# The middle attention of a two-layer graph network: a second buffer for transposed probabilities, and another order of the attention's units

## The chip, the cores and the metric

The program runs on one core of one Trainium2 chip. The metric is the device time of one execution in microseconds; several executions are timed, and their median is given. TensorE is called PE, VectorE DVE, ScalarE ACT, GpSimd POOL and SyncE SP, as in the profile.

## What is computed

The reference is a network of two layers over 625 nodes with 512 features and 20,625 edges. Each layer adds to x a graph convolution and a linear attention of its normalised input, and then a third block. The first layer's third block is the middle attention, an ordinary softmax attention over all nodes:

```python
q = (x @ wq).reshape(B, S, N_HEADS, D_K).transpose(0, 2, 1, 3)
scores = jnp.einsum('bhqd,bhkd->bhqk', q, k) / jnp.sqrt(jnp.float32(D_K))
attn = jax.nn.softmax(scores, axis=-1)
out = jnp.einsum('bhqk,bhkd->bhqd', attn, v)
return out.transpose(0, 2, 1, 3).reshape(B, S, D_MODEL) @ wo
```

It has 8 heads of 64 columns (a router picks one of three sets of weights, with 8, 4 or 1 heads of keys and values; the host repeats the columns, so that the device always computes 8). The second layer's third block multiplies the nodes by 128 matrices of 512 x 512, weighted by a softmax of distances; it takes the greater part of the time and isn't touched.

## The kernel before

All nodes stand as T = 5 tiles of P = 125 rows. Products are made in halves: an operand is split into an upper part (rounded to fp32r by ACT, names ending in h) and the rest (the difference, taken by DVE, names ending in l), and a product is three matmuls, upper by upper, upper by rest and rest by upper (L1698 to L1700).

Engines follow fixed lists written out by hand. A list of units (UNITS) sets the order in which PE fills PSUM. PSUM has four slots of two banks; unit n takes slot n % 4 (L125), and PE begins a unit when the unit that had the slot before it, four units earlier, is drained (L128 and `begin`). A unit is drained by ACT if it is a score (semaphore drained_s), and by DVE otherwise (drained_v). The semaphores count, so each engine has to keep to the order of the list.

In the middle attention there are 40 items, a tile of queries for a head each (item i is tile i % 5 of head i // 5), and three kinds of units:

- score i: six matmuls (64 rows, 314 columns) into a slot. DVE takes the negative maximum of each row (negmax, L1388), ACT the exponential into prob, which has four buffers (L967, with the sum of each row beside it), and this drains the slot. DVE corrects the sum for three padded columns (rowsum, L1393) and inverts it (rinv, L1396). POOL multiplies prob by rinv (L732).
- probT i: five transposes of prob, 125 x 125 each (L1920). ACT copies them to PTh (L978 for tiles 0 to 3, L807 for tile 4), DVE takes PTl (L1405 and, through the helper `rest`, L1124), and this drains the slot. ACT may write prob's buffer again for item i + 4 when probT i is in PSUM.
- attn h: for a head, 30 matmuls (125 rows, 314 columns) of PTh and PTl with VFh and VFl, when all five probT of the head are drained. ACT writes the result to XTh (L807), DVE to XTl (L1124), and this drains the slot.

PTh and PTl hold one head. `attention_steps(i)` gives the item whose score, the head whose product and the item whose transposes belong to step i. LAG = 2 puts the transposes two items behind the scores. The list is made from the steps, but where a step has an attention product, the scores of this and of the next step are put ahead of it, and their transposes behind it:

```python
        steps = (i, i + 1) if attention_steps(i)[1] is not None else (i,)
        for s, part in enumerate(("score", "attn", "probT")):
            ATTENTION += [(part, attention_steps(n)[s]) for n in steps if attention_steps(n)[s] is not None]
```

So PE's order around the first product is: score 6, probT 4, score 7, score 8, attn 0, probT 5, probT 6, score 9, probT 7. ACT goes through the same list, exponentials for the scores. DVE has a loop of its own (L1384): in pass i it does negmax of score i, rowsum and rinv of item i - 1, and then, for step i - 1, XTl of the head, if the step has one, and PTl of its item.

Ahead of the stage DVE pads PTh and PTl with zeros (L1382, L1383), and PE waits for it (pt_padded). Weights are loaded by SP into Wraw, one side of two (side 0 or 1), rounded by ACT into Wh (L817) and split by POOL into Wl (L687). The last weight split ahead of the stage is L1_q, on side 0. POOL does this before its first scaling. SP loads the next weights only behind the stage: the load of L1_k waits until the projection behind the attention is drained, and L1_v, the next for side 0, comes after it.

Behind the stage the projection proj1 multiplies XTh and XTl by the weight F_o, adds the result to X, and normalisation and the second layer follow.

Of the kernel before, what the change touches and what calls it, by code (L numbers as in the profile page):

```python
# [4 lines left out]
F32 = mybir.dt.float32  # L5
F32R = mybir.dt.float32r
# [3 lines left out]
ALU = mybir.AluOpType  # L10
ACT = mybir.ActivationFunctionType
# [63 lines left out]
    for i in range(n)]  # L75
UNITS += [(s + "0", i) for s, i in CONTEXT_AND_ROWS]

LAG = 2
UNITS += [("mean", 0), ("hidden", 0), ("logits", 0)] + [(s, i) for s, n in (("xt1", T), ("q1", K), ("k1", K), ("v1", 3)) for i in range(n)]
ITEMS = HEADS * T  # L80

# [1 line left out]
def attention_steps(i):  # L83


    done = i - LAG
    return (i if i < ITEMS else None, done // T - 1 if done > 0 and done % T == 0 else None,
            done if 0 <= done < ITEMS else None)

ATTENTION = []
for i in range(ITEMS + LAG + 1):
    if attention_steps(i - 1)[1] is None:
        steps = (i, i + 1) if attention_steps(i)[1] is not None else (i,)
        for s, part in enumerate(("score", "attn", "probT")):
            ATTENTION += [(part, attention_steps(n)[s]) for n in steps if attention_steps(n)[s] is not None]
UNITS += ATTENTION
UNITS += [("proj1", i) for i in range(3)]  # L100

# [79 lines left out]
def build(nc, A, out):  # L181
    with ExitStack() as ctx:
# [5 lines left out]


        X = sb("X", [P, T, D], F32)  # L190
        XN = sb("XN", [P, T, D], F32)
        XTh = sb("XTh", [128, K, NT], F32R)
        XTl = sb("XTl", [128, K, NT], F32R)
# [19 lines left out]
        with ExitStack() as s:  # L213
            sb("below_gat", [128, 3, K, D], F32, s)
            gatW = sb("gatW", [P, 3, CH, 128], F32, s)

        Wraw, Wh, Wl = ([None, None] for _ in range(3))
        for i in (1, 0):
# [1 line left out]
        rows = sb("rows", [P, 4, D], F32)  # L220
        ident = sb("ident", [128, 128], F32)
        ones = sb("ones", [128, 64], F32)
        onesr = sb("onesr", [128, 64], F32R)
        stats = sb("stats", [P, T, 6], F32)
        meanvar = sb("meanvar", [P, T, 2], F32)
        rstd = sb("rstd", [P, T], F32)
# [69 lines left out]
        with ExitStack() as s:  # L296
            QFh = sb("QFh", [128, K, NT], F32R, s)
            QFl = sb("QFl", [128, K, NT], F32R, s)
            KFh = sb("KFh", [128, K, NT], F32R, s)
            KFl = sb("KFl", [128, K, NT], F32R, s)  # L300
            VFh = sb("VFh", [P, T, D], F32R, s)
            VFl = sb("VFl", [P, T, D], F32R, s)
            PTh = sb("PTh", [P, T, NT], F32R, s)
            PTl = sb("PTl", [P, T, NT], F32R, s)
            prob = sb("prob", [P, 4, NT], F32, s)

        with ExitStack() as s:
            K2h = sb("K2h", [P, T, D], F32R, s)
# [165 lines left out]

        def slot(unit):
            return PS[:, 2 * SLOT[unit]:2 * SLOT[unit] + 2, :]

        def name_of(w):
            return WEIGHTS[w][0]
# [319 lines left out]
        def _(act):  # L799
# [155 lines left out]
            for m, tiles in enumerate(TILES):  # L955
                u = ("v1", m)
                wait_filled(u)
                upper(u, VFh[:, tiles[0]:tiles[-1] + 1], slot(u)[0:P, 0:len(tiles), :])
            weight_upper(WEIGHT["L1_q"])
            for part, n in ATTENTION:  # L960
                if part == "score":
                    item = n
                    u = ("score", item)
                    act.wait_ge(max_ready, item + 1)
                    if item >= 4:
                        act.wait_ge(filled, NUMBER[("probT", item - 4)] + 1)
                    a.activation(halves(prob[:, item % 4]), slot(u)[0:P, :, 0:HN], ACT.Exp, bias=negmax[:, item:item + 1],  # L967
                                 accum_out=rowsum[:, item:item + 1]).then_inc(drained_s, 1)
                if part == "attn":
                    head = n  # L970
                    u, o = ("attn", head), 64 * (head % 2)
                    wait_filled(u)
                    upper(u, halves(XTh[o:o + 64, head // 2]), slot(u)[o:o + 64, :, 0:HN])
                if part == "probT":
                    turned = n
                    u, c = ("probT", turned), tile_columns(turned % T)
                    wait_filled(u)
                    a.activation(PTh[:, 0:4, c], slot(u)[0:P, 0, 0:4 * P].rearrange("p (k n) -> p k n", k=4), ACT.Copy)  # L978
                    upper(u, PTh[:, 4, c], slot(u)[0:P, 1, 0:P])


            layer_std(2)
# [106 lines left out]
        def _(dve):  # L1089
# [289 lines left out]
            for m, tiles in enumerate(TILES):  # L1379
                u, j = ("v1", m), slice(tiles[0], tiles[-1] + 1)  # L1380
                rest(u, VFl[:, j], slot(u)[0:P, 0:len(tiles), :], VFh[:, j])
            v.memset(PTh[:, :, N:NT].bitcast(F32), 0.0)  # L1382
            v.memset(PTl[:, :, N:NT].bitcast(F32), 0.0).then_inc(pt_padded, 1)  # L1383
            for i in range(ITEMS + LAG + 2):  # L1384
                if i < ITEMS:
                    u = ("score", i)
                    wait_filled(u)
                    v.tensor_reduce(negmax[:, i:i + 1], slot(u)[0:P, :, 0:HN], AX.XY, ALU.max, negate=True).then_inc(max_ready, 1)  # L1388
                if 1 <= i <= ITEMS:

                    n = i - 1
                    wait_drained(dve, ("score", n))
                    v.scalar_tensor_tensor(out=rowsum[:, n:n + 1], in0=prob[:, n % 4, N - 1:N], scalar=float(N - NT),  # L1393
                                           in1=rowsum[:, n:n + 1], op0=ALU.mult, op1=ALU.add).then_inc(sum_ready, 1)
                    dve.wait_ge(sum_ready, n + 1)
                    v.reciprocal(rinv[:, n:n + 1], rowsum[:, n:n + 1]).then_inc(rinv_ready, 1)  # L1396

                _, head, turned = attention_steps(i - 1)
                if head is not None:
                    u, o = ("attn", head), 64 * (head % 2)  # L1400
                    rest(u, halves(XTl[o:o + 64, head // 2]), slot(u)[o:o + 64, :, 0:HN], halves(XTh[o:o + 64, head // 2]))
                if turned is not None:
                    u, c = ("probT", turned), tile_columns(turned % T)
                    dve.wait_ge(upper_ready, splits(u))
                    v.tensor_tensor(PTl[:, 0:4, c], slot(u)[0:P, 0, 0:4 * P].rearrange("p (k n) -> p k n", k=4),  # L1405
                                    PTh[:, 0:4, c].bitcast(F32), ALU.subtract)
                    rest(u, PTl[:, 4, c], slot(u)[0:P, 1, 0:P], PTh[:, 4, c])
            for m, tiles in enumerate(TILES):
                u, j = ("proj1", m), slice(tiles[0], tiles[-1] + 1)
                wait_filled(u)  # L1410
# [276 lines left out]
        def _(pe):  # L1687
# [201 lines left out]
            for part, n in ATTENTION:  # L1889
# [12 lines left out]
                if part == "attn":  # L1902
                    head = n
                    u, c = ("attn", head), slice(head // 2 * 128, head // 2 * 128 + 128)
                    begin(u)
                    wait_drained(pe, ("probT", T * head + T - 1))
                    for h in range(2):
                        queries = slice(h * HN, (h + 1) * HN)
                        for t in range(T):
                            ins = product(slot(u)[:, h, 0:HN], (VFh[:, t, c], VFl[:, t, c]), (PTh[:, t, queries], PTl[:, t, queries]),  # L1910
                                          t == 0, t == T - 1)
                    finish(ins)
                if part == "probT":
                    turned = n
# [216 lines left out]
```

## Time and profile before

| what | value |
|---|---|
| runs | 2633.29, 2635.6, 2635.8 us; median 2635.6 |
| profiled execution, its own time | 2621.18 us |
| its span, first to last instruction | 2619.2 us |
| middle attention, first score to first matmul of proj1 | 413.8 to 554.8 us |
| mean granted clock of TensorE over the span | 0.95 |

The profile is of one execution. Its page gives busy times by engine and the span in 40 equal slices of 65 us, with the granted clock in tenths; the trace behind it can be asked for the busy times of a stretch, for the waits of a stretch and for the instructions in order of time. Times of instructions are in us from the start of the span. TensorE's matmuls are pipelined: one starts before the one ahead of it has ended. A granted clock of 1.00 is 2.4 GHz, 0.50 is 1.2 GHz, and a value between is a mean of stretches at either.

### The profile page before, as it was taken

The numbers are of one execution on the slowest core, as the hardware profiler recorded it, in microseconds if no ns is written. First come the engines' busy times: TensorE is split into PE (matmuls) and PEld (weight loads), VectorE is DVE, ScalarE is ACT, GpSimd is POOL, SyncE is SP. The second block draws the span as 40 slices with busy tenths as digits, with TensorE's granted clock in tenths as the row PEclk, the third lists the DMA queues.
The fourth block names the chain that finished last, engine by engine and source line by source line (L and its number), as shares of the span: only waits on it lengthen the run. The fifth ranks groups of instructions, "written<-read, shape, count | busy, mean of one in ns | idle before, by whom it ended". The sixth has DMA issues, their size and how long they took to land.

```text
span 2619.2 us, 34595 instructions
## 1 busy us (share of the span) xinstructions
PE 2457.5 (94%) x11680; PEld 2056.2 (79%) x11680; DVE 1802.2 (69%) x2675; ACT 924.4 (35%) x1128; POOL 1649.6 (63%) x724
## 2 busy tenths in 40 slices
PE   6989978976899679999999999999999999999999
PEld 6878877865799667777777777777777777777777
DVE  8974324547588657777777777777777777777775
ACT  3732224522389552223223232223222322322231
POOL 0024322228888745777777777777777777777773
PEclk9989877988799779999999999999999999999999
DMA  3024010011433200221212212122122221221211
GB/s 77 16 68 162 17 65 17 1 49 47 110 87 92 79 38 33 97 84 76 96 64 96 95 65 96 69 91 96 64 96 80 80 96 64 96 91 69 96 64 36
DMA packets 49889, 190.90 MB, mean 73 GB/s; under 512 B 13300, under 2 KB 17911, under 8 KB 33444
## 3 DMA queue, kind: packets, MB, share of 16 engines
q1 hardware_dynamic: 35728, 177.90, 19.4%
q0 software_dynamic: 13200, 10.75, 1.9%
q10 hardware_dynamic: 900, 1.44, 0.2%
q8 instruction: 37, 0.61, 0.1%
q14 instruction: 24, 0.20, 0.0%
HBM read 177.54 MB, written 12.35 MB: 72 GB/s over the span
## 4 chain that ended last, share of the span: by engine, by line
PE 79%; DVE 10%; POOL 6%; issue 2%; ACT 2%; DMA 1%; SPq 0%; DVEq 0%; ACTq 0%; POOLq 0%
PE PS L1698 25%; PE PS L1700 25%; PE PS L1699 25%; POOL gatW L751 3%; POOL XN L751 2%; PE PS L1776 2%; DVE hotS L1151 1%; POOL gat L751 1%; DVE hotD L1152 1%; DVE negmax L1388 1%; DVE PTl L1405 1%; PE PS L1962 1%; PE PS L1920 0%; PE PS L1963 0%; DVE XN L1115 0%
## 5 line engine op out<-in xcount | busy, mean ns | idle before, releaser
L1648 DVE SCALAR_TENSOR_TENSOR XN<-PS,attn,XN 125x512 f32<-125x512 f32 x1083 | 805.4, 749 | 439.9 <-PE PS L1700 431.4
L789 POOL TENSOR_TENSOR OPl<-TS,OPh 128x1024 fp32r<-128x1024 f32 x256 | 677.5, 2647 | 116.7 <-ACT OPh L1061 116.7
L789 POOL TENSOR_TENSOR OPl<-RAW,OPh 128x1024 fp32r<-128x1024 f32 x192 | 555.2, 2892 | 273.4 <-ACT OPh L1061 273.4
L1698 PE MATMUL PS<-OPh,XTh 128*125 128x512 f32 x1280 | 507.6, 397 | 2.0 <-DVE attn L1602 2.0
L1700 PE MATMUL PS<-OPh,XTl 128*125 128x512 f32 x1280 | 506.1, 395 | 0.0
L1699 PE MATMUL PS<-OPl,XTh 128*125 128x512 f32 x1280 | 503.7, 394 | 0.0
L1061 ACT ACTIVATE OPh<-TS 128x1024 fp32r<-128x1024 f32 x256 | 271.8, 1062 | 530.0 <-PE PS L1700 517.3
L1061 ACT ACTIVATE OPh<-RAW 128x1024 fp32r<-128x1024 f32 x192 | 203.8, 1062 | 579.1 <-PE PS L1700 579.1
L1698 PE MATMUL PS<-OPh,Sh 128*125 128x512 f32 x1024 | 404.3, 395 | 3.1 <-DVE XN L1645 3.1
L1700 PE MATMUL PS<-OPh,Sl 128*125 128x512 f32 x1024 | 403.4, 394 | 0.0
L1699 PE MATMUL PS<-OPl,Sh 128*125 128x512 f32 x1024 | 402.1, 393 | 0.0
L1699 PEld LDWEIGHTS PS<-OPl,XTh 128*125 128x125 f32 x1280 | 238.7, 187 | 60.4
L1700 PEld LDWEIGHTS PS<-OPh,XTl 128*125 128x125 f32 x1280 | 238.0, 186 | 61.2
L1698 PEld LDWEIGHTS PS<-OPh,XTh 128*125 128x125 f32 x1280 | 237.5, 186 | 60.1 <-DVE attn L1602 2.2
L687 POOL TENSOR_TENSOR Wl<-Wraw,Wh 128x2048 fp32r<-128x2048 f32 x15 | 69.2, 4615 | 255.0 <-ACT Wh L817 254.9
L1698 PEld LDWEIGHTS PS<-OPh,Sh 128*125 128x125 f32 x1024 | 189.5, 185 | 50.6 <-issue 3.9
L1962 PE MATMUL PS<-hotE,msgh 125*128 125x314 f32 x660 | 201.5, 321 | 28.8 <-DVE msgl L1506 21.6
L1700 PEld LDWEIGHTS PS<-OPh,Sl 128*125 128x125 f32 x1024 | 190.0, 186 | 48.1
L1699 PEld LDWEIGHTS PS<-OPl,Sh 128*125 128x125 f32 x1024 | 190.1, 186 | 47.7
L1963 PE MATMUL PS<-hotE,msgl 125*128 125x314 f32 x660 | 198.9, 316 | 0.0
L1962 PEld LDWEIGHTS PS<-hotE,msgh 125*128 125x128 f32 x660 | 130.2, 197 | 32.5 <-issue 29.1
L751 POOL DMA_INDIRECT gatW<-nodes,dstI x90 | 134.8, 1497 | 29.0 <-issue 27.1
(345 smaller groups left out, 3587.6 us busy)
## 6 DMA issues: line engine op xcount, KB each, us to landing
RAW<-in_values SPq DMA_DIRECT2D x64, 2048.0 KB, 7.5
filters<-filt SPq DMA_DIRECT2D x14, 672.0 KB
fil<-filters SPq DMA_DIRECT2D x11, 840.0 KB
Wraw<-in_ffn SPq DMA_DIRECT2D x4, 1024.0 KB, 5.3
Wraw<-in_L_q SPq DMA_DIRECT2D x2, 1024.0 KB, 5.1
Wraw<-in_L_k SPq DMA_DIRECT2D x2, 1024.0 KB, 8.7
Wraw<-in_L_v SPq DMA_DIRECT2D x2, 1024.0 KB, 7.3
gatW<-nodes,dstI POOLq DMA_INDIRECT x90
```

The lines of the kernel that those rows point to most:

```text
L687: g.tensor_tensor(Wl[SIDE[w]][:], Wraw[SIDE[w]][:], Wh[SIDE[w]][:].bitcast(F32), ALU.subtract).then_inc(w_split, 1)
L751: g.indirect_dma_start(gats[c % RING][:, u, :], None, nodes, bass.IndirectOffsetOnAxis(ap=dstI[:, t:t + 1], axis=0)).then_inc(gathered[c % ...
L789: g.tensor_tensor(OPl[:, j], operand_source(j, parity), OPh[:, j].bitcast(F32), ALU.subtract).then_inc(op_lower, 1)
L1061: a.activation(OPh[:, j], operand_source(j, parity), ACT.Copy).then_inc(op_upper, 1)
L1151: v.tensor_scalar(hotS[:, parity, u, :], iota16[:, 0:N + 1], srcF[:, bass.ds(t, 1)], None, ALU.is_equal)
L1648: v.scalar_tensor_tensor(out=XN[:, t], in0=PS[0:P, bank, :], scalar=w, in1=XN[:, t], op0=ALU.mult, op1=ALU.add).then_inc(v_added, 1)
L1698: mm(dst, lh, rh, start=start, stop=False, skip_group_check=resumed)
L1699: mm(dst, lh, rl, start=False, stop=False, skip_group_check=resumed)
L1700: return mm(dst, ll, rh, start=False, stop=stop, skip_group_check=resumed)
L1776: ins = mm(PS[0:P, count_bank(n), 0:HALF], hotS[:, parity, u, s * P:(s + 1) * P], hotD[:, parity, u, 0:HALF], start=(c == m * COUNT_CHUNKS ...
L1962: mm(dst, msgh[:, q, u, c_], hot, start=(first and u == 0), stop=False)
L1963: ins = mm(dst, msgl[:, q, u, c_], hot, start=False, stop=(last and u == EB - 1))
```

## The change

1. LAG is 3, and the product of a head belongs to the step one later than before: its five probT come three items behind the scores, and the product one item behind the last of them.
2. The pairs of scores are gone: every step is score, attn, probT. The order around the first product is: score 7, probT 4, score 8, probT 5, score 9, attn 0, probT 6, score 10, probT 7, score 11.
3. PTh and PTl have two buffers. Even heads use PTh and PTl, odd heads PTh_odd and PTl_odd for tiles 0 to 3, and PTh_odd4 and PTl_odd4 for tile 4. PTh_odd lies over XN, which isn't in use in the stage. PTh_odd4 and PTl_odd4 lie over Wraw of side 0. So ACT (ahead of its first exponential) and DVE (ahead of the padding) wait until L1_q is split. To make room onesr has 2 columns instead of 64 (two are used).
4. DVE pads both buffers, with eight memsets instead of two. Its loop is one pass longer.

```diff
-LAG = 2
+LAG = 3
 def attention_steps(i):
-    done = i - LAG
-    return (i if i < ITEMS else None, done // T - 1 if done > 0 and done % T == 0 else None,
-            done if 0 <= done < ITEMS else None)
-ATTENTION = []
-for i in range(ITEMS + LAG + 1):
-    if attention_steps(i - 1)[1] is None:
-        steps = (i, i + 1) if attention_steps(i)[1] is not None else (i,)
-        for s, part in enumerate(("score", "attn", "probT")):
-            ATTENTION += [(part, attention_steps(n)[s]) for n in steps if attention_steps(n)[s] is not None]
+    turned = i - LAG
+    behind = turned - 1
+    return (i if i < ITEMS else None, behind // T - 1 if behind > 0 and behind % T == 0 else None,
+            turned if 0 <= turned < ITEMS else None)
+ATTENTION_STEPS = ITEMS + LAG + 2
+ATTENTION = [(part, n) for i in range(ATTENTION_STEPS)
+             for part, n in zip(("score", "attn", "probT"), attention_steps(i)) if n is not None]
...
         X = sb("X", [P, T, D], F32)
+        with ExitStack() as s:
+            PTh_odd = sb("PTh_odd", [P, T - 1, NT], F32R, s)
         XN = sb("XN", [P, T, D], F32)
...
+        with ExitStack() as s:
+            sb("below_PT", [128, 3, K, D], F32, s)
+            PTh_odd4 = sb("PTh_odd4", [P, NT], F32R, s)
+            PTl_odd4 = sb("PTl_odd4", [P, NT], F32R, s)
...
-        onesr = sb("onesr", [128, 64], F32R)
+        onesr = sb("onesr", [128, 2], F32R)
...
+        def prob_turned(head):
+            if head % 2:
+                return (PTh_odd[:], PTh_odd4[:]), (PTl_odd[:], PTl_odd4[:])
+            return (PTh[:, 0:T - 1], PTh[:, T - 1]), (PTl[:, 0:T - 1], PTl[:, T - 1])
...
             weight_upper(WEIGHT["L1_q"])
+            act.wait_ge(w_split, WEIGHT["L1_q"] + 1)
             for part, n in ATTENTION:
...
-            v.memset(PTh[:, :, N:NT].bitcast(F32), 0.0)
-            v.memset(PTl[:, :, N:NT].bitcast(F32), 0.0).then_inc(pt_padded, 1)
-            for i in range(ITEMS + LAG + 2):
+            dve.wait_ge(w_split, WEIGHT["L1_q"] + 1)
+            for head in range(2):
+                for first, last in prob_turned(head):
+                    v.memset(first[:, :, N:NT].bitcast(F32), 0.0)
+                    ins = v.memset(last[:, N:NT].bitcast(F32), 0.0)
+            ins.then_inc(pt_padded, 1)
+            for i in range(ATTENTION_STEPS + 1):
```

The copies on ACT, the subtractions on DVE and the matmuls of the product take their tiles from `prob_turned` instead of from PTh and PTl, in the same shapes.

## Rows read from the trace of the kernel before

**Rows 1.** The page: TensorE's busy time and granted clock in 40 slices

```profile
PE 2457.5 (94%) x11680; PEld 2056.2 (79%) x11680; DVE 1802.2 (69%) x2675; ACT 924.4 (35%) x1128; POOL 1649.6 (63%) x724
...
PEclk9989877988799779999999999999999999999999
```

**Rows 2.** Busy times by engine and granted clock (PEclk), by head

```profile
core 0: us, PE busy (x) PEld busy (x) DVE busy (x) ACT busy (x) POOL busy (x), PEclk, DMA share, GB/s
...
420.40:438.50 18.10, 17.62 (x61) 14.86 (x61) 9.25 (x28) 8.49 (x22) 4.66 (x7) 0.50 0.00 0
...
455.70:470.60 14.90, 13.29 (x85) 11.72 (x85) 9.79 (x28) 8.39 (x21) 4.12 (x6) 1.00 0.01 2
...
485.20:501.50 16.30, 14.85 (x85) 13.26 (x86) 9.67 (x27) 8.39 (x21) 3.98 (x6) 0.90 0.00 0
...
501.50:516.10 14.60, 13.33 (x85) 11.76 (x85) 9.51 (x27) 8.26 (x21) 3.93 (x5) 1.00 0.01 2
...
532.40:547.20 14.80, 11.27 (x61) 10.28 (x61) 7.06 (x19) 5.85 (x15) 2.40 (x4) 0.76 0.00 1
```

**Rows 3.** The waits of the stretch 413 to 556 us

```profile
PE PS L1698 <- DVE PTl L1124: 6.9, 8, 1.8
```

**Rows 4.** All engines in order of time, the start of the stage

```profile
413.65 0.07 DVE L1383 MEMSET PTl<- 125x15 f32 x1
...
413.77 0.40 PE L1698 MATMUL PS<-KFh,QFh 64*125 64x314 f32 x1 [1.46 <-DVE PTl L1383]
...
414.82 4.53 POOL L687 TENSOR_TENSOR Wl<-Wraw,Wh 128x2048 fp32r<-128x2048 f32 x1 [9.22 <-ACT Wh L817]
...
420.61 1.38 PE L1920 MATMUL PS<-ident,prob 125*125 125x125 f32 x5 [3.98 <-POOL prob L732]
```

**Rows 5.** PE in order of time at half clock, and the first attention product

```profile
431.53 0.62 PE L1698 MATMUL PS<-KFh,QFh 64*125 64x314 f32 x1
...
433.39 1.41 PE L1920 MATMUL PS<-ident,prob 125*125 125x125 f32 x5
...
434.73 0.62 PE L1698 MATMUL PS<-KFh,QFh 64*125 64x314 f32 x1
...
436.46 0.46 PE L1698 MATMUL PS<-KFh,QFh 64*125 64x314 f32 x1
...
438.69 0.60 PE L1698 MATMUL PS<-PTh,VFh 125*128 125x314 f32 x1 [0.46 <-DVE PTl L1124]
...
445.69 1.25 PE L1920 MATMUL PS<-ident,prob 125*125 125x125 f32 x10
```

**Rows 6.** PE in order of time at full clock, a product and what follows

```profile
470.64 0.38 PE L1698 MATMUL PS<-PTh,VFh 125*128 125x314 f32 x1 [0.76 <-DVE PTl L1124]
...
475.07 1.25 PE L1920 MATMUL PS<-ident,prob 125*125 125x125 f32 x10
...
476.26 0.40 PE L1698 MATMUL PS<-KFh,QFh 64*125 64x314 f32 x1
...
477.31 0.81 PE L1920 MATMUL PS<-ident,prob 125*125 125x125 f32 x5
...
478.05 0.41 PE L1698 MATMUL PS<-KFh,QFh 64*125 64x314 f32 x1
```

**Rows 7.** ACT and DVE in order of time behind the same product

```profile
475.27 0.69 ACT L807 ACTIVATE XTh<-PS 64x628 fp32r<-64x628 f32 x1 [3.16 <-PE PS L1700]
...
475.99 0.80 DVE L1124 TENSOR_TENSOR XTl<-PS,XTh 64x628 fp32r<-64x628 f32 x1 [4.52 <-ACT XTh L807]
...
477.50 0.79 DVE L1388 TENSOR_REDUCE negmax<-PS 125x1 f32<-125x628 f32 x1
...
478.48 0.66 DVE L1405 TENSOR_TENSOR PTl<-PS,PTh 125x500 fp32r<-125x500 f32 x1
...
479.25 0.80 DVE L1388 TENSOR_REDUCE negmax<-PS 125x1 f32<-125x628 f32 x1
```

**Rows 8.** PE in order of time, the last transposes

```profile
542.93 0.88 PE L1920 MATMUL PS<-ident,prob 125*125 125x125 f32 x5 [1.47 <-POOL prob L732]
```

More of the change, by code:

```diff
@@ L305, in build @@
             prob = sb("prob", [P, 4, NT], F32, s)
+            PTl_odd = sb("PTl_odd", [P, T - 1, NT], F32R, s)
         with ExitStack() as s:
@@ L977, in _ @@
                     wait_filled(u)
-                    a.activation(PTh[:, 0:4, c], slot(u)[0:P, 0, 0:4 * P].rearrange("p (k n) -> p k n", k=4), ACT.Copy)
-                    upper(u, PTh[:, 4, c], slot(u)[0:P, 1, 0:P])
+                    (first, last), _ = prob_turned(turned // T)
+                    a.activation(first[:, :, c], slot(u)[0:P, 0, 0:4 * P].rearrange("p (k n) -> p k n", k=4), ACT.Copy)
+                    upper(u, last[:, c], slot(u)[0:P, 1, 0:P])
             layer_std(2)
@@ L1404, in _ @@
                     dve.wait_ge(upper_ready, splits(u))
-                    v.tensor_tensor(PTl[:, 0:4, c], slot(u)[0:P, 0, 0:4 * P].rearrange("p (k n) -> p k n", k=4),
-                                    PTh[:, 0:4, c].bitcast(F32), ALU.subtract)
-                    rest(u, PTl[:, 4, c], slot(u)[0:P, 1, 0:P], PTh[:, 4, c])
+                    (first_h, last_h), (first_l, last_l) = prob_turned(turned // T)
+                    v.tensor_tensor(first_l[:, :, c], slot(u)[0:P, 0, 0:4 * P].rearrange("p (k n) -> p k n", k=4),
+                                    first_h[:, :, c].bitcast(F32), ALU.subtract)
+                    rest(u, last_l[:, c], slot(u)[0:P, 1, 0:P], last_h[:, c])
             for m, tiles in enumerate(TILES):
@@ L1906, in _ @@
                     wait_drained(pe, ("probT", T * head + T - 1))
+                    (first_h, last_h), (first_l, last_l) = prob_turned(head)
                     for h in range(2):
@@ L1909, in _ @@
                         for t in range(T):
-                            ins = product(slot(u)[:, h, 0:HN], (VFh[:, t, c], VFl[:, t, c]), (PTh[:, t, queries], PTl[:, t, queries]),
-                                          t == 0, t == T - 1)
+                            right = (last_h[:, queries], last_l[:, queries]) if t == T - 1 else (first_h[:, t, queries], first_l[:, t, queries])
+                            ins = product(slot(u)[:, h, 0:HN], (VFh[:, t, c], VFl[:, t, c]), right, t == 0, t == T - 1)
                     finish(ins)
```

## The prediction, made before the changed kernel ran

> **What bounds the kernel now.** I read the page first: TensorE is busy 94% of the span, and the granted clock falls below full in the first 15 of the 40 slices only [rows 1]. The change touches one stage there, the middle attention. The busy times cut at the beginnings of the attention products (438.5, 455.7, 470.6, 485.2, 501.5, 516.1, 532.4, 547.2 us) give one head per stretch [rows 2]. Three heads at full clock take 14.6 to 14.9 us, with PE 13.3 us busy (two of them are in the rows); two that hold a stretch of half clock (0.90 granted; one is in the rows) take 16.3. From 420.4 to 438.5 the clock is 0.50 throughout, though PE is busy for 17.6 of 18.1 us. So PE is nearly the bound, and what counts is its few gaps and the clock they leave behind. The list of waits names the largest regular one: eight attention products wait 6.9 us in all for the last PTl on VectorE [rows 3].
>
> **The change, part by part.**
>
> **1. The start.** The new buffers for the fifth tile lie over Wraw[0], so VectorE's padding now waits until POOL has split L1_q, and PE waits for the padding. POOL's split runs from 414.82 to 419.35; today the first score starts at 413.77, well before [rows 4]. After the change it starts at about 419.8: the end of the split, then eight small memsets (the one shown takes 0.07 us, and they overlap) and two semaphores. ScalarE waits for the same split; even if it loads its table of exponentials only then, that lies beside the first score and its maximum. Today PE has done three scores by 416.6 and waits until 420.61 for the first transposes [rows 4]. After, it has done none by 419.8, but has no gap from there on: with three scores ahead, the first transposes find their probabilities ready. It runs at half clock, as it does today from 420.4, because it stood idle for longer.
>
> At half clock a score takes 1.86 us ahead of transposes (431.53 to 433.39), some 1.70 ahead of another score (434.73 to 436.46), and five transposes take 1.34 [rows 5]. Ahead of the first attention product now stand ten scores and six transposes: 4 x 1.70 + 6 x 1.86 + 6 x 1.34 = 26.0 us, so it begins at 445.8, not 438.7: **7.1 us later**. One score and one set of transposes in that are work brought forward.
>
> **2. A head at full clock.** Call the end of an attention product 0, and let it be the one behind score 9. At full clock the product takes 4.43 us (470.64 to 475.07), five transposes behind it 0.60 (ten took 1.19), a score 1.05, transposes behind a score 0.74 [rows 6]. VectorE's item is 1.75 us (negmax to negmax; 0.98 of it for negmax, rowsum and rinv, 0.77 for PTl), XTl is 0.80 and ScalarE's XTh ahead of it 0.69 [rows 7]. Now the order. PE issues transposes 6, score 10, transposes 7, score 11. PSUM has four slots in turn, so score 11 takes the slot of the attention product, and that is free when VectorE has written XTl. VectorE's list for that step says negmax of score 10 first, then rowsum, rinv, and only then XTl. Before the change the extra score of the pair stood ahead of the product, so its maximum was taken while the product ran, and XTl came first. Without pairs: score 10 is complete at 0.60 + 1.05 + 0.10 = 1.75; negmax, rowsum and rinv 0.98, XTl 0.80 give 3.53 (XTh is done long before); with 0.15 of semaphore, as from VectorE's XTl at other places, score 11 starts at 3.7. PE was through with transposes 7 at 0.60 + 1.05 + 0.74 = 2.4. That is **a new PE gap of 1.3 us, once a head, right behind the product**. The double buffer does let VectorE do one more PTl during the product, but four items and XTl remain before the next one: 3.53 + 0.77, a wait for score 11 to 4.85, three items of 1.75 and one or two short waits of 0.2 to 0.3 for slots, so 10.3 to 10.7. With the product 14.7 to 15.2 a head, against 14.6 to 14.9. On the timetable alone the second buffer earns nothing, because the slot and the order of VectorE's list take back what it gives.
>
> **3. The clock.** What prices the gap is the clock. In the head from 420.4 to 438.5, PE issued scores and transposes without a break at half clock, and the clock did not come back; it came back during the attention product that followed [rows 2, 5]. At full clock PE waited 0.76 us ahead of six products, as in rows 6, and the clock fell at three of these, one of them in the head of 0.90 [rows 2]; it fell again in the last head, where the gap between transposes was 1.47 us and the granted clock of the head 0.76 [rows 2, 8]. The new gap is 1.3 us, close to the last, and lies among the same kind of work, scores and transposes. So I expect the clock to fall once behind each product, near the gap, and then to stay at half, since nothing but scores and transposes follows until the next product. Today the fall comes just before a product and is repaired by it within 3 to 4 us, for 1.4 to 1.7 us a time; after the change it comes at the other end of the head, and PE, not VectorE, sets the pace.
>
> The Trainium skill, TensorE: Matmul & The Clock Gate, "A second HAM failure mode: psum-queue depth-cycling", tells of a kernel that cycled through its PSUM banks and waited briefly between groups of matmuls, whose clock went back and forth; its rule gives the sum below, and its absence the first rival's. This trace agrees with it so far as one gap can show it.
>
> **The sum.** A head in that state: 3.7 us to score 11, which I leave at full clock (1.05), then three scores and three transposes at half clock, 3 x 1.86 + 3 x 1.34 = 9.6, less 0.16 since the last score has no transposes behind it: 14.2, and 14.1 for what still runs fast. The product, half of it slow, took 7.0 us in the first head (438.69 to 445.69) [rows 5]; where the fall came at its start a head was 1.6 us longer, so 6.0. I take 6.4. Head: **20.5 us**. Six of these from product 0 to product 6: 123.0, against 93.9 today (438.5 to 532.4). From product 6 to product 7 all probabilities are already scaled: product 6.4, XTh 0.7, XTl 0.8, four PTl 3.2, semaphores 0.2, so 11.3 against 14.8 [rows 2]. Behind product 7 nothing changes. Sum: 7.1 + (123.0 - 93.9) + (11.3 - 14.8) = **+32.7 us**.
>
> Costed at nothing: the shrunken onesr (two of its columns are all that is read); the other addresses of PTh and PTl (same shapes, same engines); SyncE, whose next load into Wraw[0] is L1_v, queued behind the wait for the last proj1, after the attention; POOL, which scales in the same order and is idle for most of the stage.
>
> The profiled execution took 2621.18 us (span 2619.2), the median of the runs is 2635.6, 14.4 us more. I carry the difference over to the median and take 32 of it for runs whose clock falls otherwise today: **2668 us**.
>
> **Rivals.**
>
> *The clock holds.* For: at full clock PE is still busy most of the time around the new gap, and three of six gaps of 0.76 us did nothing. Against: 1.47 us was enough once. Then only the timetable counts: product 0 at +7.1; the first interval 17.2 + 0.5, five of 15.2 (76.0), two falls as today 3.2, which brings product 6 to 542.7; then 4.4 + 5.0 to product 7 at 552.1, against 547.2. So +5, or +2 without any fall: 2637 to 2641. If it falls in some heads only, each that is spared gives back 20.5 - 15.2 = 5.3 us: two to four spared make 2647 to 2657.
>
> *Faster.* The place is score 11's slot. If it were free in time, VectorE (9.6 us a head) would no longer stand before PE, whose own work is 5 x 1.79 + 4.43, less 0.15, 13.2 us. Then product 1 comes 15.6 behind product 0, five more at 13.2, then 9.4: 445.8 + 15.6 + 66.0 + 9.4 = 536.8, against 547.2, or -10: 2625. It decides this way only if XTl is done by 2.4 us behind the product's end, and by rows 6 and 7 it is done at 3.53. The Trainium skill, Trainium Kernel Development and Optimization, "Best Practices", advises double buffers for performance; by it this rival would be the likely one, but in its sense PSUM's slots and VectorE's order would have to be widened too.
>
> *The start costs less.* If the split of L1_q ended earlier than in this trace, the first product would come up to 4 us sooner. That is a term of the forecast's own range and has no effect on the sign.
>
> **How the numbers follow.** Half clock behind nearly every product: 0.78, at +32 with its own range 2657 to 2674 (one or two heads spared below; every head 0.5 longer and the runs' own spread above). Some heads spared, 2647 to 2657: 0.07. The clock holds: 0.11. Faster: 0.04. The range from 2649 to 2674 leaves out the last two and a little of each end. A measurement of this kernel can tell about 0.2% (5.3 us) from no change: faster 0.04, the clock that holds gives 0.09 of no change and 0.02 of slower, so slower is 0.87.
>
> **What would show it.** Right: the first score near 419.8 and the first product near 446; a wait of PE for XTl of about 1.3 us some seven times, as scores (L1698) released by DVE XTl; granted clock about 0.65 over the stage; products some 20.5 us apart; the stage ending some 32 us later, nothing else moved. Wrong: products 15 us apart at a clock near 0.95 (the first rival), or no wait for XTl and PE without gaps (the second). An unexpected wait of an exponential for its prob buffer would mean that I misread the order of the lists.

## The result and the profile after

| | before | after |
|---|---|---|
| median of the runs, us | 2634.4 (4 runs) | 2664.9 (4 runs) |
| ratio of the times, 95% interval | | 1.0133 [1.0105, 1.0161] |
| profiled execution, its own time, us | 2621.2 | 2674.3 |
| mean granted clock over its span | 0.950 | 0.931 |
| last weight load of the stage ahead to first matmul of proj1, us | 411.7 to 554.8 (143.2) | 422.1 to 600.3 (178.1) |
| first attention product behind that weight load, us | 27.0 | 33.7 |
| product 0 to product 6, us | 93.8 | 124.4 |
| product 6 to product 7, us | 14.8 | 11.0 |

The changed kernel is 30.5 us slower by the medians. The forecast was 2668 with a range from 2649 to 2674. The weight load belongs to the last matmul of the stage ahead, which starts 0.2 us behind it; below, "the stage" is counted from this load to the first matmul of proj1. TensorE's busy time and its granted clock on the page, against [rows 1]:

```profile
PE 2506.8 (94%) x11680; PEld 2098.6 (79%) x11680; DVE 1800.7 (67%) x2681; ACT 924.2 (35%) x1128; POOL 1654.0 (62%) x724
...
PEclk9988777669699887999999999999999999999999
```

TensorE has as many instructions as before and is busy 49 us longer: the same work at a lower clock. The eighth and ninth slice (468 to 601 us) show a clock of 6 and 6, where those of before (458 to 589 us) show 9 and 8. The busy times by head (the columns are those of [rows 2]; the first stretch runs from the first score to product 0, the last from product 6 to product 7):

```profile
core 0: us, PE busy (x) PEld busy (x) DVE busy (x) ACT busy (x) POOL busy (x), PEclk, DMA share, GB/s
430.00:455.80 25.80, 25.75 (x90) 22.21 (x90) 13.11 (x35) 12.89 (x31) 6.32 (x8) 0.50 0.00 1
455.80:476.50 20.70, 19.57 (x87) 17.21 (x86) 9.77 (x26) 8.26 (x21) 3.95 (x5) 0.66 0.00 0
476.50:497.30 20.80, 19.52 (x86) 17.24 (x85) 9.98 (x26) 8.38 (x21) 3.95 (x5) 0.66 0.00 1
580.30:591.30 11.00, 8.60 (x52) 8.27 (x51) 6.01 (x16) 4.12 (x11) 1.58 (x2) 0.81 0.00 0
```

A head that took 14.6 to 17.2 us takes 20.6 to 20.9, with the same 85 or so matmul records. PE is idle for 1.1 to 1.3 us of it, no more than the 1.3 to 1.6 of before; but the clock is 0.66 where it was 0.83 to 1.00. PE's waits in the stage name the idle time (the engine and line that waits, what it waited for; total, times, longest):

```profile
PE PS L1716 <- DVE PTl_odd L1399: 7.3, 1, 7.3
PE PS L1716 <- DVE XTl L1137: 7.2, 6, 1.3
PE PS L1716 <- DVE PTl_odd L1137: 2.4, 1, 2.4
```

The eight waits for the last PTl ahead of a product [rows 3] are gone but for one of 2.4 us ahead of product 7. In their place stand one wait at the start (7.3 us, for the padding, which waits for POOL's split) and six waits for XTl. The start, all engines in order of time:

```profile
425.26 4.49 POOL L698 TENSOR_TENSOR Wl<-Wraw,Wh 128x2048 fp32r<-128x2048 f32 x1 [9.23 <-ACT Wh L828]
429.82 0.07 DVE L1398 MEMSET PTh<- 125x12 f32 x1 [5.71 <-POOL Wl L698]
...
430.05 0.62 PE L1716 MATMUL PS<-KFh,QFh 64*125 64x314 f32 x1 [7.29 <-DVE PTl_odd L1399]
```

And the place of the regular wait, PE in order of time around the end of the first product, then ACT's XTh and DVE beside it:

```profile
455.84 0.63 PE L1716 MATMUL PS<-PTh,VFh 125*128 125x314 f32 x1
...
462.57 0.70 PE L1939 MATMUL PS<-ident,prob 125*125 125x125 f32 x5
463.20 0.41 PE L1716 MATMUL PS<-KFh,QFh 64*125 64x314 f32 x1
...
464.26 0.81 PE L1939 MATMUL PS<-ident,prob 125*125 125x125 f32 x5
466.20 0.41 PE L1716 MATMUL PS<-KFh,QFh 64*125 64x314 f32 x1 [1.13 <-DVE XTl L1137]
...
468.19 0.62 PE L1716 MATMUL PS<-KFh,QFh 64*125 64x314 f32 x1
```

```profile
462.76 0.69 ACT L818 ACTIVATE XTh<-PS 64x628 fp32r<-64x628 f32 x1 [5.10 <-PE PS L1718]
...
464.37 0.81 DVE L1405 TENSOR_REDUCE negmax<-PS 125x1 f32<-125x628 f32 x1 [6.58 <-PE PS L1718]
465.10 0.15 DVE L1410 SCALAR_TENSOR_TENSOR rowsum<-prob,rowsum 125x1 f32<-125x1 f32 x1
465.28 0.16 DVE L1413 RECIPROCAL rinv<-rowsum 125x1 f32<-125x1 f32 x1
465.36 0.78 DVE L1137 TENSOR_TENSOR XTl<-PS,XTh 64x628 fp32r<-64x628 f32 x1
```

XTh was written by 463.45, so DVE could have taken XTl from then on. It stood idle until score 10 was in PSUM (464.37), because its list has that score's maximum ahead of XTl. Score 11, at 466.20, is the unit that needs the product's slot. The first matmul of that score still takes 0.41 us; that of the next score (468.19) takes 0.62, its length at half clock. The granted clock went to half at 467.8 and came back at 481.4, within the next product (from 476.5), and so behind each of the first six products: half from 467.8 to 481.4, 488.2 to 501.9, 508.7 to 522.4, and so on.

Outside the stage the two profiled executions differ by another 18 us: 10.4 ahead of it and 7.8 behind it. Ahead of it TensorE ran at half clock for 71.7 us before and 92.1 after. In the profiles below that figure lies anywhere from 68.2 to 88.8, both for kernels made from the kernel before (68.2 to 88.8) and for those made from the changed one (71.7 to 88.8), so it isn't put down to the change here. Comparisons of traces below are therefore of the stage alone. The kernel before was timed beside each group of experiments, each group on another chip: its medians were 2633.7 us (experiments 1 to 4), 2630.1 (5 to 8) and 2635.1 (9). Between groups, and against the changed kernel's runs above (beside 2634.4), the ratios are therefore the safer comparison.

### The profile page after: what moved, and what is told of

Read it like the earlier page. It is cut to its first block, busy times and chain, and to the rows that moved or that the text cites. A ratio compares the mean times of both kernels' runs of the same rounds, so it can differ in the third digit from the quotient of the medians.

```text
span 2672.5 us, 34602 instructions
## 1 busy us (share of the span) xinstructions
PE 2506.8 (94%) x11680; PEld 2098.6 (79%) x11680; DVE 1800.7 (67%) x2681; ACT 924.2 (35%) x1128; POOL 1654.0 (62%) x724
## 4 chain that ended last, share of the span: by engine, by line
PE 81%; DVE 9%; POOL 6%; issue 2%; ACT 1%; DMA 1%; SPq 0%; DVEq 0%; ACTq 0%; POOLq 0%
PE PS L1716 26%; PE PS L1718 25%; PE PS L1717 25%; POOL gatW L762 3%; POOL XN L762 2%; PE PS L1939 1%; DVE hotS L1164 1%; PE PS L1794 1%; DVE hotD L1165 1%; POOL gat L762 1%; PE PS L1981 1%; PE PS L1982 0%; DVE XN L1128 0%; DVE full L1457 0%; DVE XTl L1137 0%
## 5 line engine op out<-in xcount | busy, mean ns | idle before, releaser
L800 POOL TENSOR_TENSOR OPl<-TS,OPh 128x1024 fp32r<-128x1024 f32 x256 | 678.2, 2649 | 118.6 <-ACT OPh L1074 118.6
```

Of the source, the lines that this page charges most:

```text
L800: g.tensor_tensor(OPl[:, j], operand_source(j, parity), OPh[:, j].bitcast(F32), ALU.subtract).then_inc(op_lower, 1)
```

## The experiments

The theory: the order of VectorE's list (maximum of score 10 ahead of XTl) makes a gap in PE behind each product, the gap lowers the clock, and the stage's sparse work doesn't bring it back until the next product. The rivals: the loss lies in the late start; or in the lost pairs as such; or in the gaps' own length rather than the clock. Each line below gives the median, the ratio to the kernel before with its 95% interval, and the stage in the profiled execution (before 143.2 us, after 178.1).

**1. XTl first.** The changed kernel, with VectorE's XTl taken ahead of the maximum of the same pass. Nothing else is altered.

```diff
             for i in range(ATTENTION_STEPS + 1):
+                _, head, turned = attention_steps(i - 1)
+                if head is not None:
+                    u, o = ("attn", head), 64 * (head % 2)
+                    rest(u, halves(XTl[o:o + 64, head // 2]), slot(u)[o:o + 64, :, 0:HN], halves(XTh[o:o + 64, head // 2]))
                 if i < ITEMS:
...
-                _, head, turned = attention_steps(i - 1)
-                if head is not None:
-                    u, o = ("attn", head), 64 * (head % 2)
-                    rest(u, halves(XTl[o:o + 64, head // 2]), slot(u)[o:o + 64, :, 0:HN], halves(XTh[o:o + 64, head // 2]))
                 if turned is not None:
```

> The changed kernel with one edit: in VectorE's loop XTl of the head stands ahead of the maximum of the next score, not behind it. Theory (the slot of the attention product is freed late, PE waits 1.3 us for it, and that wait lets the clock fall): XTl is done some 1.8 us behind the product's end, before PE asks for the slot at 2.4, so no PE wait for XTl, the clock stays at full from the first product on, heads of 13.5 to 14 us, the stage some 38 us shorter than in the changed kernel: about 2627, faster than the kernel before. First rival (the late start and the deeper lag cost the time, the clock falls for another reason): the clock still falls behind every product, heads stay at 20 us or more, 2655 to 2665. Second rival (timetable only, the clock plays no part): heads lose 1.3 us each, 2656.

Measured: 2626.5 us over 10 runs, 0.9971 [0.9949, 0.9992]; stage 135.7. PE and DVE behind the first product, then two heads:

```profile
459.43 0.70 PE L1939 MATMUL PS<-ident,prob 125*125 125x125 f32 x5
460.06 0.41 PE L1716 MATMUL PS<-KFh,QFh 64*125 64x314 f32 x1
...
461.12 0.81 PE L1939 MATMUL PS<-ident,prob 125*125 125x125 f32 x5
461.86 0.41 PE L1716 MATMUL PS<-KFh,QFh 64*125 64x314 f32 x1
```

```profile
460.34 0.80 DVE L1137 TENSOR_TENSOR XTl<-PS,XTh 64x628 fp32r<-64x628 f32 x1 [5.85 <-ACT XTh L818]
461.23 0.81 DVE L1409 TENSOR_REDUCE negmax<-PS 125x1 f32<-125x628 f32 x1
```

```profile
468.80:482.70 13.90, 13.47 (x86) 11.78 (x85) 9.81 (x26) 8.37 (x22) 3.96 (x5) 1.00 0.00 1
482.70:496.50 13.80, 13.51 (x86) 11.81 (x85) 9.76 (x26) 8.24 (x22) 3.93 (x6) 1.00 0.00 1
```

Score 11 starts 2.4 us behind the product's end and waits for nothing; the clock stays full from 458.0 to the end of the stage. One moved block of VectorE's list takes 38 us off the changed kernel, and this version is a little faster than the kernel before. The late start is still in it (product 0 stands 33.7 us behind the last weight load of the stage ahead, as in the changed kernel), so the start is not the main loss. Two longer waits are still in it too, around product 7, and the clock didn't fall there:

```profile
545.75 0.78 PE L1939 MATMUL PS<-ident,prob 125*125 125x125 f32 x5 [1.22 <-POOL prob L743]
...
548.37 0.38 PE L1716 MATMUL PS<-PTh_odd,VFh 125*128 125x314 f32 x1 [1.84 <-DVE PTl_odd L1137]
```

**2. The pairs gone, and nothing else.** The kernel before, with its list made plainly from the steps (LAG 2, one buffer).

```diff
-ATTENTION = []
-for i in range(ITEMS + LAG + 1):
...
+ATTENTION = [(part, n) for i in range(ITEMS + LAG + 1)
+             for part, n in zip(("score", "attn", "probT"), attention_steps(i)) if n is not None]
```

> The kernel before with one part of the change: the pairs of scores are gone, LAG stays 2, one buffer, no wait for the split. Theory: the score three units behind each product then waits for XTl behind a maximum, as in the changed kernel, so the clock falls behind every product here too; on top of it PE waits for the last PTl ahead of the product, about 1.8 us. Heads of 21 to 23 us, 2670 to 2685. Rival (the second buffer or the start behind the split costs the time): within 10 us of the kernel before, about 2640.

Measured: 2677.6 us over 4 runs, 1.0174 [1.0131, 1.0216]; stage 189.6, heads of 22.7 to 22.9 us. Its waits:

```profile
PE PS L1694 <- DVE PTl L1120: 16.1, 8, 2.0
...
PE PS L1694 <- DVE XTl L1120: 10.0, 8, 1.6
```

Without pairs and without a second buffer PE waits ahead of every product, and again behind each of the first seven (1.1 to 1.3 us; the eighth wait for XTl, 1.6 us, is that of proj1). The second buffer with its one item more of lag removes the first row (one such wait is left, 2.4 us at the end); it doesn't touch the second.

**3. The pairs put back.** The changed kernel (LAG 3, two buffers) with the paired construction of the kernel before.

```diff
-ATTENTION = [(part, n) for i in range(ATTENTION_STEPS)
-             for part, n in zip(("score", "attn", "probT"), attention_steps(i)) if n is not None]
+ATTENTION = []
+for i in range(ATTENTION_STEPS):
+    if attention_steps(i - 1)[1] is None:
+        steps = (i, i + 1) if attention_steps(i)[1] is not None else (i,)
...
```

> The changed kernel with the pairs of scores put back: two scores, the product, two sets of transposes; two buffers, LAG 3 and the wait for the split stay. The wait for XTl moves from a score to a set of transposes one unit later, but the exponential of the second score now waits for the transposes behind the product (four prob buffers), so two waits of about 0.6 us take the place of one of 1.3. Theory: the clock falls behind some products only; heads between 14 and 18 us, 2635 to 2655. Rival (the pairs play no part): as the changed kernel, 2665.

Measured: 2646.1 us over 10 runs, 1.0044 [1.0019, 1.0068]; stage 157.6. PE's waits in it:

```profile
PE PS L1720 <- ACT prob L983: 2.9, 6, 0.5
...
PE PS L1943 <- DVE XTl L1141: 2.1, 6, 0.4
PE PS L1943 <- DVE PTl L1141: 1.9, 3, 0.6
PE PS L1943 <- DVE PTl_odd L1141: 1.8, 3, 0.6
```

The pairs do bring XTl forward (0.4 us of waiting instead of 1.2), and take back over half of the loss. But three short waits now stand in each head, and the clock still fell at some of them: half at 463.8 to 474.1, 498.0 to 508.2, 518.4 to 525.3 and 549.2 to 559.4. (A last one, 566.2 to 573.1, belongs to the wait of 2.4 us ahead of product 7.) The order within VectorE's list is the better repair.

**4. The gap filled.** The changed kernel, with nine matmuls more ahead of the transposes in front of score 11. Their result is used by nothing (the transposes overwrite it). VectorE's order and the time at which XTl is ready stay as they are; PE only has work instead of a gap.

```diff
                     pe.wait_ge(prob_ready, turned + 1)
+                    if T <= turned < ITEMS - LAG and turned % T == 2:
+                        for _ in range(9):
+                            mm(slot(u)[0:P, 0, 0:HN], QFh[:, 0, 0:P], KFh[:, 0, 0:HN], start=True, stop=True)
                     for t in range(T):
```

> The changed kernel with nine extra matmuls (128 rows, 314 columns, results not used) ahead of the second set of transposes behind each of the first six products, where PE would otherwise wait. The timetable is the same: score 11 still waits for XTl until 3.7 us behind the product. It tells the clock's part from the gap's own. Theory (the clock is the price): the clock stays full once the first product has raised it, heads of 15.2 us, the stage about 28 us shorter than in the changed kernel: about 2638. Rival (the gap and the order cost the time by themselves): no faster than the changed kernel, 2665 to 2675.

Measured: 2636.3 us over 10 runs, 1.0013 [0.9998, 1.0027]; stage 142.6. PE behind the product that began at 469.3, then two heads:

```profile
475.38 1.58 PE L1939 MATMUL PS<-KFh,QFh 128*125 128x314 f32 x9
476.80 0.71 PE L1942 MATMUL PS<-ident,prob 125*125 125x125 f32 x5
477.47 0.40 PE L1716 MATMUL PS<-KFh,QFh 64*125 64x314 f32 x1
```

```profile
469.30:484.40 15.10, 14.76 (x94) 13.04 (x95) 9.85 (x27) 8.46 (x22) 3.96 (x5) 1.00 0.00 1
484.40:499.60 15.20, 14.81 (x95) 13.18 (x95) 9.74 (x27) 8.43 (x22) 3.96 (x5) 1.00 0.01 1
```

A head is 15.1 to 15.2 us at full clock. Score 11 begins 3.8 us behind the product's end (477.47 - 473.70), 0.1 later than in the changed kernel, so this is the timetable of the changed kernel without its fall of the clock. The 28.6 us between the medians of the two (by the ratios about 32) are put down to the clock. This version can't be told from the kernel before. The gap's own length costs 1.2 to 1.3 us a head against the 13.9 of experiment 1, about what the kernel before loses by waits of its own; what follows it costs another 5.5.

**5. The padding of the second buffer late.** The changed kernel; head 0's buffer is padded at once, head 1's (whose fifth tile lies over Wraw) when its first transposes come.

```diff
-            act.wait_ge(w_split, WEIGHT["L1_q"] + 1)
...
+                    if turned == T:
+                        act.wait_ge(w_split, WEIGHT["L1_q"] + 1)
...
-            dve.wait_ge(w_split, WEIGHT["L1_q"] + 1)
-            for head in range(2):
...
+            pad(0)
...
+                    if turned == T:
+                        dve.wait_ge(w_split, WEIGHT["L1_q"] + 1)
+                        pad(1)
...
                     wait_drained(pe, ("probT", T * head + T - 1))
+                    if head == 1:
+                        pe.wait_ge(pt_padded, 2)
```

> The changed kernel with the start undone: only the even buffer is padded ahead of the stage, the odd one ahead of its first use, and ScalarE waits for the split of L1_q only ahead of item 5. It prices the start alone. Theory: the first product comes some 6 us earlier (20.6 us of wait for the first transposes as before, four scores done by then, 19.2 us of scores and transposes at half clock), all else stays, the clock falls behind each product: 2659. Rival (the start lowers the clock for the whole stage): the falls behind the products go too, below 2645.

Measured: 2657.4 us over 4 runs, 1.0098 [1.007, 1.0126]; stage 169.5. Its first product stands 28.2 us behind the last weight load of the stage ahead instead of 33.7, and the heads are unchanged:

```profile
416.80:442.90 26.10, 22.96 (x91) 19.48 (x91) 15.40 (x35) 13.88 (x32) 10.88 (x9) 0.63 0.00 1
442.90:463.50 20.60, 19.47 (x86) 17.17 (x85) 9.85 (x30) 8.26 (x21) 3.95 (x5) 0.67 0.00 0
```

In the traces the start is worth 5.5 us. The medians differ by 7.5 us and the ratios by 0.0035 (about 9 us), but the intervals of the two ratios overlap, so the times alone don't fix its size. The stage is 8.6 us shorter: besides the start, the clock held behind product 7 in this profile, where it had fallen in the changed kernel's. PE still waits at the start, 1.5 and 3.1 us, and is at half clock from 423.5 to 447.4.

**6. Both: XTl first and the padding late** (edits 1 and 5 together).

> Both edits together: XTl ahead of the maximum, and the late padding. The two terms should add: heads of 13.9 us, the first product some 6 us earlier than with XTl first alone: 2620. Rival (the start's cost is hidden or the clock at the start decides otherwise): as XTl first alone, 2626.

Measured: 2627.5 us over 12 runs (2613.5 to 2635.2), 0.9985 [0.997, 1.0001]; stage 131.3, against 135.7 of the first experiment. The stage is 4.4 us shorter in the traces (the first product 5.6 us earlier, and 1.5 us lost again behind product 7, where the clock fell from 540.1 to 543.5). But the expected sum, 2620, isn't in the medians: 2627.5 against 2626.5, which is the rival's number. The runs of both spread over some 20 us, so this comparison is inconclusive.

**7. The kernel before with no pairs and XTl first** (edits 2 and 1 on the kernel before: LAG 2, one buffer). It asks whether the order of VectorE's list alone would do.

> The kernel before without pairs (one buffer, LAG 2), with XTl ahead of the maximum. It tells what the second buffer and the deeper lag are worth once the slot is freed early. Theory: no wait for XTl, but the product still waits about 1.8 us for the last PTl right ahead of it, where the clock falls now and then and is repaired by the product: heads of 15 to 16.5 us, no start behind the split: 2630 to 2643, slower than XTl first with two buffers plus its late start would be in steady state (13.9 us a head). Rival (the buffer is worth nothing, the order of VectorE's list is everything): heads of 13.9 us, 2620.

Measured: 2651.5 us over 10 runs, 1.0068 [1.0048, 1.0087]; stage 161.5. A miss: it is 8 us above the upper end of what was expected. Its waits (the one left for XTl is that of proj1) and a head:

```profile
PE PS L1694 <- DVE PTl L1120: 16.1, 8, 2.0
...
PE PS L1916 <- POOL prob L728: 9.8, 15, 4.0
PE PS L1694 <- DVE XTl L1120: 1.6, 1, 1.6
```

```profile
468.60:486.40 17.80, 14.95 (x86) 13.29 (x86) 9.83 (x26) 8.38 (x21) 3.97 (x5) 0.89 0.00 1
```

The waits for XTl are gone as in the first experiment, but a wait of 2.0 us for PTl (1.8 at the last) stands ahead of every product. The clock falls at each of products 1 to 6, for 3.4 us (twice 6.9), where "now and then" was expected; and in these heads stand two more waits of 0.3 to 0.5 us each for POOL's prob, which the expectation didn't have. In the head shown PE is idle for 2.9 us. Against the first experiment (heads of 13.9 us) this gives the worth of the second buffer with one item more of lag, once the slot is free in time: 3.9 us a head, 25 us in the medians. The buffer is useful; the order of the list hid that.

**8. The clock kept at the start.** Experiment 6, with 8 matmuls without use ahead of the first score and 18 ahead of the first transposes, where PE otherwise waits.

```diff
+            begin(("score", 0))
+            wait_drained(pe, ("k1", K - 1))
+            for _ in range(8):
+                mm(slot(("score", 0))[0:P, 0, 0:HN], QFh[:, 0, 0:P], KFh[:, 0, 0:HN], start=True, stop=True)
             pe.wait_ge(pt_padded, 1)
...
+                    if turned == 0:
+                        for _ in range(18):
+                            mm(slot(u)[0:P, 0, 0:HN], QFh[:, 0, 0:P], KFh[:, 0, 0:HN], start=True, stop=True)
                     pe.wait_ge(prob_ready, turned + 1)
```

> As both edits together, with 8 extra matmuls (128 rows, 314 columns, results not used) ahead of the first score and 18 ahead of the first transposes, where PE waits. It tells whether the long stretch at half clock ahead of the first product is a debt of PE's waits at the start. Theory (as behind the products: a wait among scores and transposes lets the clock fall, and they don't bring it back): the clock holds or comes back before the first transposes, the first product comes 7 to 9 us earlier, 2612. Rival (scores and transposes alone let it fall, wait or not): the clock falls all the same and the extra matmuls cost 0 to 3 us, 2620 to 2623.

Measured: 2615.2 us over 6 runs, 0.9938 [0.9916, 0.9959]; stage 121.6. From the end of the stage ahead to product 0, and the first head:

```profile
421.50:442.10 20.60, 19.52 (x121) 16.64 (x119) 16.56 (x42) 14.97 (x32) 10.94 (x9) 1.00 0.00 1
442.10:455.90 13.80, 13.55 (x86) 11.82 (x86) 9.64 (x30) 8.22 (x22) 3.95 (x5) 1.00 0.00 1
```

The first product stands 20.5 us behind the stage's beginning, where it was 28.1 in experiment 6 and 33.7 in the changed kernel: scores and transposes go on at full clock if they begin at it. This is the fastest version: by the ratio 16 us faster than the kernel before, by the medians 12.3 us faster than experiment 6 and 50 us faster than the changed kernel.

**9. The kernel before, with its gap filled.** Five matmuls without use (the product overwrites their result) ahead of each product, while PE waits for the last PTl.

```diff
                     begin(u)
+                    for _ in range(5):
+                        mm(slot(u)[0:P, 0, 0:HN], QFh[:, 0, 0:P], KFh[:, 0, 0:HN], start=True, stop=True)
                     wait_drained(pe, ("probT", T * head + T - 1))
```

> The kernel before with five extra matmuls (128 rows, 314 columns, results not used) ahead of each attention product, where PE waits 0.76 us for the last PTl. It tells whether the falls of the kernel before have the same cause. Theory: no fall at the products, heads of 14.7 us throughout, the fall in the last head stays, the stage 3 to 6 us shorter, 2626 to 2632 where the kernel before is at 2632. Rival (those falls have another cause, or come by themselves): falls at two or three products as before, the stage no shorter, 2632 to 2636.

Measured: 2623.2 us over 10 runs, 0.9966 [0.9946, 0.9986]; stage 138.5. A head of it:

```profile
455.20:469.90 14.70, 14.00 (x92) 12.46 (x91) 9.64 (x27) 8.39 (x21) 3.97 (x6) 1.00 0.01 2
```

All of its heads from the second to the sixth take 14.6 or 14.7 us, the undisturbed length of the kernel before. So that kernel's own falls at the products [rows 2] come from its waits of 0.76 us, as far as one profile of each shows, and it too can be had faster. The gain by the ratio, 9 us with an interval from 4 to 14, is more than the 3 to 6 us expected; the stage is 4.7 us shorter, and whether the rest is more than the spread of the runs stays open.

## Why the prediction was right

**The start.** Forecast: first score at 419.8, first product 7.1 us later. The first score began 7.9 us behind the last weight load of the stage ahead (before 2.1), the first product 33.7 (before 27.0), 6.7 us later. The stretch between was 25.8 us at a clock of 0.50, forecast 26.0. The cause was the named one: the memsets follow the split within 0.1 us. Experiment 5 takes 5.5 us of it away in the trace (28.2 instead of 33.7).

**The gap.** Forecast: 1.3 us, score 11 at 3.7 us behind the product's end, held by XTl behind the maximum of score 10. Measured: 466.20 - 462.57 = 3.63 us, waits of 1.1 to 1.3 us. From the end of XTl (466.14) to the score it was 0.06 us, where the sum had 0.15. I wrote "some seven times" and it was six: behind the last product but one there are no scores left. The timetable without the clock was forecast at 14.7 to 15.2 us a head; experiment 4 measured 15.1 to 15.2. That the order of the list is the cause is shown by experiment 1.

**The clock.** Forecast: a fall behind each product, half clock until the next product, 20.5 us a head and a clock of about 0.65. Measured: 20.6 to 20.9 and 0.66. Product 0 to product 6 took 124.4 us, forecast 123.0. The product was forecast at 6.4 us; it went from 6.7 down to 6.2 over these six, 6.5 in the mean. From its end to the next product was forecast at 14.1; it went from 13.9 up to 14.7, 14.3 in the mean. The two drift together with the clock: the fall came 5.2 us behind the end of product 0 and only 4.6 behind product 5, and the return moved from 4.9 us behind the start of product 1 to 3.5 us behind that of product 6.

This step rested on thin ground, as its chance of 0.78 says: one wait of 1.47 us had lowered the clock once. That it fell six times out of six bears the forecast out here, and experiments 1 and 4 show that the wait is the cause. But waits about as long or longer at the end of the stage left the clock alone in some profiles (1.22 and 1.84 us in experiment 1; 2.4 us in 4 and 5), so a wait of this length isn't enough by itself to foretell a fall. The passage of the Trainium skill that I cited ("TensorE: Matmul & The Clock Gate", "A second HAM failure mode: psum-queue depth-cycling") held in kind: it tells of a clock that goes back and forth through brief waits between groups of matmuls, and here one brief wait a head did it, six times.

**The end.** Product 6 to product 7: 11.0 us, forecast 11.3. "Behind product 7 nothing changes" was wrong by 1.4 us: that part took 9.0 instead of 7.6, because the clock was at half from 590.6 to 597.5.

**The sum.** +6.7 + 30.6 - 3.8 + 1.4 = +34.9 us in the stage, forecast +32.7. The medians differ by 30.5. Why they differ by some 4 us less than the stage does in the two traces isn't settled. The stage came out 2.2 us longer than forecast, the difference of the medians smaller; that the forecast of the time is as near as 3 us is in part luck.

**The rivals.** *The clock holds* is what experiment 4 made by force: 2636.3, and the rival said 2637 to 2641. *Faster* was to decide by XTl being done by 2.4 us behind the product's end. In experiment 1 it is done at 1.7 (461.14 - 459.43), score 11 starts at 2.4, and the time is 2626.5 where the rival said 2625; the first head has 16.3 us for its 15.6. The other heads are 13.8 to 14.0 us, not 13.2: PE is busy for 13.5 and not quite without gaps. The advice of double buffers (the Trainium skill, "Trainium Kernel Development and Optimization", "Best Practices") gives the overlap of DMA with compute as its purpose. The prediction stretched it to a buffer between engines, and no run here tests the advice as it stands there. What the runs show of this buffer, together with its item more of lag: it didn't pay in the changed kernel, and it pays as soon as the product's slot is drained in time (experiment 7 against 1).

## What to carry to other kernels

When a second buffer takes a wait away, look for the next thing that the same engine needs behind that place, here a PSUM slot whose drain stood behind the next score's maximum in another engine's list, and move that drain ahead of work that can wait. Price a short wait of TensorE by what runs behind it: the gap cost 1.2 us a head by itself, and the 13.6 us at half clock that followed cost another 5.5. Where a short wait can't be removed, matmuls without use in its place are worth a trial, in a slot that is free anyway.

## What the runs showed of the hardware

- Work that kept the clock didn't bring it back. Scores (64 rows, 314 columns) and transposes ran at half clock without a break for 25.8 us after the change, PE busy for 25.75, and the clock stayed at 0.50. The same units ran at a clock of 1.00 for 20.6 us in experiment 8, where PE came to them at full clock and was given matmuls of 128 rows in its two waits. I had the first half from the kernel before; the second was not in any row I had.
- The same length of wait doesn't always act alike. Six waits of 1.1 to 1.3 us behind a product lowered the clock six times. The waits of 2.0 us ahead of products 1 to 6 in experiment 7 lowered it each time, but only for 3.4 to 6.9 us; it came back within the product. In experiment 3 waits of 0.3 to 0.6 us were enough in some heads and not in others. Around product 7 a pair of waits of 1.22 and 1.84 us left the clock full in experiment 1, and the same pair was followed by a fall in experiment 6 (540.1 to 543.5); the wait of 2.4 us there went with a fall in the changed kernel and in experiment 3, and with none in experiments 4 and 5. What tells these apart isn't settled.
- Added matmuls made three kernels faster: 28.6 us (experiment 4 against the changed kernel, by the medians), 12.3 us (8 against 6) and, by the ratio 0.9966 [0.9946, 0.9986], 9 us (9 against the kernel before).
- The runs of one kernel spread by very different amounts: about 20 us in experiments 1, 6 and 9, 6 us in the ten runs of experiment 4, 10 us in the four of the changed kernel. Half-clock time ahead of the stage lay anywhere from 68.2 to 92.1 us in the profiles, though neither the change nor an experiment alters the work there. The 4.4 us that experiment 6 gained in its stage didn't show in medians of 10 and 12 runs.
